# Cross-attention and mixture-of-experts kernel: one-time work of the first batch reordered, shared expert's first products moved among the last batches' second half

## The chip, the cores and the metric

One core of one Trainium2 chip. Time is device microseconds (us) of one launch; less is better. The engines are PE (TensorE, matmuls and transposes), DVE (VectorE), ACT (ScalarE), POOL (GpSimd) and SP (SyncE, which only issues DMAs here). Each has its own instruction stream, written out by hand, and they meet only at semaphores.

## The reference

There are 16 batches of 128 rows of 512 numbers. Each batch passes a cross-attention over 128 context rows (32 heads of 16, rotary positions), and the result is added to the stream. Then a feed-forward layer of one shared expert and 16 routed ones, of which each row takes its two best, is added.

```python
def _swiglu(x, a, b, c):
    return jax.nn.silu(x @ a.T) * (x @ b.T) @ c.T
# attention
q = (x @ Wq).reshape(b, n, N_HEADS, HEAD_DIM)
k, v = jnp.split(ctx @ Wkv, 2, axis=-1)
q = apply_axial_rope(q, pos_map)
k = apply_axial_rope(k, ctx_pos_map)
w = jax.nn.softmax(logits, axis=-1)          # logits = q k^T * scale
attn @ Wout + bout
# feed-forward
shared_output = _swiglu(x, shared_w1, shared_w3, shared_w2)
scores = jax.nn.sigmoid(x @ gate_w.T)
_, topk_idx = jax.lax.top_k(scores + bias, K)
for e in range(E):
    routed_output = routed_output + combine[:, e:e + 1] * _swiglu(x, w1[e], w3[e], w2[e])
# the whole
x = x + attention(layernorm(x), ctx_1024, positions)
x = x + feed_forward(layernorm(x))
```

## The kernel before

Every fp32 product with a weight is made of three fp16 products of a high and a low part. ACT makes the high part of a weight (`weights_high`, `split_shared`: a scaled copy), DVE the low part (`weights_low`, `w13_low`, `w2_low`: the difference). The parts of activations are made in the same way by ACT and by DVE or POOL.

The attention is a software pipeline over batches. `pipeline(step, engine, first, last, ...)` runs `step(b)` for b = 0, 1, 2 and so on, and `on(d, part)` inside it runs that part for batch b + d, if there is such a batch; `ahead` names parts of batch 0 that were issued before the loop. So in step b PE projects k and v of batch b, projects q of batch b - 1 and turns its halves (`stack_transpose`, four groups g; p_st is their one buffer), makes scores, maxima, shifted scores and the weighed values of batch b - 2, the output projection of batch b - 3 (`project_out`), and the transposed second norm and the gate's logits of batch b - 4 (`xn2_transpose`, `gate_logits`). The order of the parts inside a step is fixed for each engine. Batches are counted 0 to 15 here (B = 16), and the last steps, after 15, only drain: PE works to step B + 3 = 19, DVE likewise, ACT and POOL to step 20.

Ahead of the pipeline stands one-time work. SP loads x of batch 0, Wkv, context 0, Wq, context 1, x of batch 1, Wout, x of batches 2 to 15 in one DMA of 3.6 MB (`stream[:, 2:B]`, semaphore `x_late`), the gate's weights and, after two waits, contexts 2 and 3. POOL issues the DMAs of the positions (8 bytes a piece) and of `bout`. DVE normalises batch 0, splits Wkv, splits Wq, clears `negmax`, `hidden` and the value buffer, waits for the positions, makes the angles, waits for ACT's sines and scales the tables; only then does it enter step 0 and 1, in which `k_turn(0)` and `k_sum(0)` rotate the keys. `project_q(0)` on PE waits for `k_turn(0)`, because q and k share the buffer p_qk. Wout is split at the end of step 1, the gate's weights at the end of step 2.

At the seam to the feed-forward part, `split_shared` splits the shared expert's weights in step B + 2 = 18 on ACT and DVE, into `used_twice_too`, which holds keys, queries and values until then. When PE has done step 19 and all logits are kept, it makes the first gate and up products (`gate_up(0, ...)`), and then the slots n = 0 to 15 of the shared expert follow, two to a `pair(j)`: `hidden_transpose(n)`, the gate and up products of n + 1, `down(n)`. PE adds `count()` behind slot 3 (COUNTED) and `place()` behind slot 10 (TABLED); both serve the routing, whose DVE work (`routing_work`) lies beside slots 0 to 11. ACT loads the rows of slot n + 2 with a DMA when the products of slot n + 1 are made (`load_rows`). DVE's first `y_take(0)` waits until SP's first store to `out` has landed, which SP issues when the rows of all batches are stored.

Then 31 tiles at most of two times 128 rows go through the routed experts (slots 16 and on): rows are gathered by POOL, weights loaded by SP, outputs added to `out` by POOL.

## Time and profile before

| | |
|---|---|
| median of 3 runs | 739.29 us (738.96 to 743.66) |
| profiled execution | 740.43 us, of which the span of instructions is 738.7 us |
| mean granted PE clock of the profiled execution | 0.976 of full speed |

The profiled execution's time holds 1.7 us beside its span. The rows from its trace are shown below. Times in them count from the start of the span.

### The profile page before, as it was taken

The numbers are of one execution on the slowest core, as the hardware profiler recorded it, in microseconds if no ns is written. First come the engines' busy times: TensorE is split into PE (matmuls) and PEld (weight loads), VectorE is DVE, ScalarE is ACT, GpSimd is POOL, SyncE is SP. The second block draws the span as 40 slices with busy tenths as digits, with TensorE's granted clock in tenths as the row PEclk, the third lists the DMA queues.
The fourth block names the chain that finished last, engine by engine and source line by source line (L and its number), as shares of the span: only waits on it lengthen the run. The fifth ranks groups of instructions, "written<-read, shape, count | busy, mean of one in ns | idle before, by whom it ended". The sixth has DMA issues, their size and how long they took to land.

```text
span 738.7 us, 20567 instructions
## 1 busy us (share of the span) xinstructions
PE 681.3 (92%) x7616; PEld 436.3 (59%) x7616; DVE 525.3 (71%) x992; ACT 397.6 (54%) x666; POOL 366.1 (50%) x439
## 2 busy tenths in 40 slices
PE   3389999999999999998489998999999999999992
PEld 1156666666666666666245665666666666666661
DVE  5968888888888888876537772467676666767671
ACT  4255666665666666665521111366666656666661
POOL 5455556655556665542100001145776557777662
PEclk9789999999999999999979999999999999999997
DMA  9610111000011110000113256258568875555952
GB/s 300 222 48 9 37 38 39 34 21 35 21 35 35 35 35 28 28 29 31 59 57 100 72 182 225 73 145 250 97 192 239 254 199 94 98 94 78 278 121 31
DMA packets 37601, 73.88 MB, mean 100 GB/s; under 512 B 3920, under 2 KB 8048, under 8 KB 37552
## 3 DMA queue, kind: packets, MB, share of 16 engines
q1 hardware_dynamic: 26736, 48.81, 19.2%
q0 software_dynamic: 8800, 20.73, 14.9%
q10 hardware_dynamic: 2016, 3.67, 1.7%
q8 instruction: 33, 0.54, 0.3%
q14 instruction: 16, 0.13, 0.1%
HBM read 69.85 MB, written 22.81 MB: 125 GB/s over the span
## 4 chain that ended last, share of the span: by engine, by line
PE 83%; DVE 6%; DMA 4%; issue 3%; POOL 2%; ACT 1%; POOLq 0%; SPq 0%; DVEq 0%; ACTq 0%
PE p_sc L712 13%; PE p_qk L692 13%; PE p_sc L692 12%; PE p_v L486 8%; PE p_qk L486 7%; PE p_pv L586 5%; PE p_st L534 4%; PE p_pv L589 4%; PE p_sc L566 3%; PE p_sc L549 3%; PE p_pv L596 2%; PE p_tr L678 2%; PE p_v L699 2%; PE p_sc L569 2%; DMA xeT<-xn2T_dram 2%
## 5 line engine op out<-in xcount | busy, mean ns | idle before, releaser
L809 ACT ACTIVATE prob<-p_sc 128x512 f32<-128x512 f32 x128 | 71.4, 601 | 58.8 <-PE p_sc L569 58.8
L1073 DVE TENSOR_REDUCE negmax<-p_sc 128x4 f16<-128x512 f32 x128 | 82.7, 685 | 8.6 <-PE p_sc L549 8.0
L924 ACT CAST hiddenT<-p_v 128x384 f16<-128x384 f32 x54 | 25.9, 479 | 108.7 <-PE p_v L699 108.7
L712 PE MATMUL p_sc<-used_twice,hiddenT 128*128 128x512 f16 (+1 forms) x342 | 80.1, 379 | 0.0
L1192 DVE TENSOR_TENSOR hidden<-p_sc,act_g 128x352 f32<-128x352 f32 x55 | 28.8, 524 | 68.5 <-PE p_sc L692 47.0
L1467 POOL COPY from_at<-from_rows 128x1 uint32 (+1 forms) x40 | 33.0, 825 | 89.0 <-DVE from_rows L1309 85.8
L692 PE MATMUL p_sc<-used_twice,xeT 128*128 128x352 f16 x468 | 76.2, 313 | 0.0
L692 PE MATMUL p_qk<-used_twice,xeT 128*128 128x352 f16 x468 | 76.2, 312 | 0.0
L1487 POOL DMA_INDIRECT out<-prob,to_at x38 | 67.8, 1786 | 11.0 <-issue 10.1
L1100 DVE SCALAR_TENSOR_TENSOR used_twice<-w,used_twice 128x704 f16<-128x704 f32 x80 | 67.7, 887 | 2.5
L692 PEld LDWEIGHTS p_sc<-used_twice,xeT 128*128 128x128 f16 x468 | 45.8, 98 | 24.0
L486 PE MATMUL p_qk<-used_twice,xnT 128*128 128x512 f16 x192 | 51.7, 396 | 8.5 <-issue 8.5
L912 ACT COPY xeT<-p_tr 128x1024 f16<-128x1024 f16 x40 | 40.5, 1013 | 34.2 <-PE p_tr L678 33.8
L933 ACT ACTIVATE used_twice<-w 128x704 f16<-128x704 f32 x80 | 58.6, 783 | 0.0
L692 PEld LDWEIGHTS p_qk<-used_twice,xeT 128*128 128x128 f16 x468 | 45.7, 98 | 20.5
L1446 POOL TENSOR_TENSOR xn_parts<-xn,xn_parts 128x512 f16<-128x512 f32 x16 | 18.5, 1156 | 70.8 <-ACT xn_parts L836 70.8
L586 PE MATMUL p_pv<-prob,used_twice_too 128*32 128x128 f32 x1024 | 52.6, 277 | 0.5 <-DVE attn L1092 0.5
L1209 DVE TENSOR_SCALAR prob<-p_sc,gate_at 128x512 f32<-128x512 f32 x38 | 28.5, 751 | 33.4 <-PE p_sc L712 30.8
L589 PE MATMUL p_pv<-prob,sum_row 128*32 128x128 f32 x1024 | 51.5, 273 | 0.0
L712 PEld LDWEIGHTS p_sc<-used_twice,hiddenT 128*128 128x128 f16 (+1 forms) x342 | 31.8, 98 | 31.5
L486 PE MATMUL p_v<-used_twice,attnT 128*128 128x512 f16 x192 | 47.6, 380 | 2.0 <-POOL attnT L1442 2.0
L1472 POOL DMA_INDIRECT xe<-xn_dram,from_at x40 | 45.4, 1135 | 8.1 <-issue 3.6
(186 smaller groups left out, 1551.3 us busy)
## 6 DMA issues: line engine op xcount, KB each, us to landing
w<-e SPq DMA_DIRECT2D x20, 1408.0 KB
w<-e SPq DMA_DIRECT2D x20, 512.0 KB
out<-stream SPq DMA_DIRECT2D x17, 256.0 KB, 2.1
xn_dram<-xn_parts SPq DMA_DIRECT2D x16, 256.0 KB, 2.0
xn2T_dram<-xn2T SPq DMA_DIRECT2D x16, 256.0 KB, 2.0
w<-e SPq DMA_DIRECT2D x20, 192.0 KB
stream<-x SPq DMA_DIRECT2D x1, 3584.0 KB, 16.8
xeT<-xn2T_dram ACTq DMA_DIRECT2D x14, 256.0 KB, 2.7
```

The lines of the kernel that those rows point to most:

```text
L486: mm = pe.matmul(to, rows[:, r_part, c, :], w[:, w_part, c, :], start=(c == 0 and r_part + w_part == 0), stop=(c == last and r_part == 1))
L586: pe.matmul(p_pv[2 * HD * n:2 * HD * (n + 1), block], vpad[:, par, head(c, n), :], prob[:, c % RING, n * P:(n + 1) * P], start=(c % 4 == 0 ...
L589: mm = pe.matmul(pv_sum[2 * HD * n:2 * HD * (n + 1), :], sum_row[:, c % 4, :], prob[:, c % RING, n * P:(n + 1) * P], start=False, stop=(c ...
L692: mm = pe.matmul(p_out, xeT[:, u, x_part, c, :], w[:, w_part, c, at:at + INNER], start=(c == 0 and x_part + w_part == 0), stop=(c == KC - ...
L712: mm = pe.matmul(p_y[u][:], hiddenT[0:k, h_part, c, :], w[0:k, w_part, c, :], start=(c == 0 and h_part + w_part == 0), stop=(c == len(ICH) ...
L809: act.activation(prob[:, c % RING, :], p_scored(c)[:], ACT.Exp, scale=SCALE).then_inc(exp_ready, 1)
L912: act.copy(xeT[:, u], p_xT).then_inc(sems.xeT_ready, 1)
L933: act.activation(split[par][0][:, 0, c], w13[:, par, c], ACT.Copy, scale=W_SCALE).then_inc(hi13, 1)
L1073: dve.tensor_reduce(negmax[:, c % 2, at:at + CH], p_scored(c)[:].rearrange("p (h t) -> p h t", t=P), AX_X, ALU.max, negate=True).then_inc( ...
L1100: dve.scalar_tensor_tensor(to[0][:, 1, c], w13[:, par, c], W_SCALE, to[0][:, 0, c], ALU.mult, ALU.subtract).then_inc(lo13, 1)
L1472: pool.indirect_dma_start(out=xe[:, u].rearrange("p a d -> p (a d)"), out_offset=None, in_=xn2_dram, in_offset=bass.IndirectOffsetOnAxis(a ...
L1487: pool.indirect_dma_start(out=out, out_offset=bass.IndirectOffsetOnAxis(ap=to_at[:, par, u:u + 1], axis=0), in_=ye[:, par, u], in_offset=N ...
```

## The change

In the first batch:

- POOL's DMA of the positions goes to ACT's queue, from an array laid out by row, so each of the 128 pieces is one run of 128 bytes.
- DVE clears its buffers first, before x has landed, makes the angles behind the first norm and ahead of the split of Wkv, and splits Wq after the tables; `k_turn(0)` and `k_sum(0)` are issued before step 0. ACT makes the sines ahead of its copies of Wq.
- Wout is split at the end of step 2 in place of step 1. `bias_add` goes one step later, with the wait for `bout` ahead of its first call only.
- SP loads context 2 ahead of the large DMA of x, with two waits before it.

At the seam:

- The shared expert's split weights stand in `used_twice`, where the projections' weights were. Their places with `wo16`, `parts` and the routing tables are exchanged. They are split in three places: gate and up weights on ACT at the end of step 17, on DVE half there and half in step 18, the down weights in step 18.
- PE leaves the pipeline after step 17. It makes the first gate product, spreads the last sums, makes the first up product, and then does `xn2_transpose(14)` and `project_out(15)`. `gate_logits(14)`, `xn2_transpose(15)` and `gate_logits(15)` go into slots 0 and 1, with the work of DVE and ACT that belongs to them.
- `p_u`, `p_hT`, `p_rank`, `p_total` and `p_table` change their PSUM buffers.
- The routing's DVE work begins two slots later, its last piece (`tables`) one slot later; `count()` stands behind slot 5 and `place()` behind slot 11. SP loads the rows of slots 0 and 1 in step 12 in place of step 15.

```diff
-COUNTED, TABLED = 3, 10
+COUNTED, TABLED = 5, 11
-        split = {0: split_in(used_twice[:, 0:each]), 1: split_in(used_twice[:, each:2 * each]),
-                 "shared": split_in(used_twice_too[:, 0:each])}
+        split = {0: split_in(used_twice_too[:, 0:each]), 1: split_in(used_twice[:, each:2 * each]),
+                 "shared": split_in(used_twice[:, 0:each])}
...
             sp.dma_start(wo_in, wo.rearrange("(c p) n -> p c n", p=P)).then_inc(w_o, 16)
+            sp.wait_ge(ctx_lo, 1)
+            sp.wait_ge(ctx_loaded, 2 * 16)
+            sp.dma_start(ctx_sb[:, 0], ctxT[2].rearrange("(c p) t -> p c t", p=P)).then_inc(ctx_loaded, 16)
             sp.dma_start(stream[:, 2:B, :], x_t[:, 2:B, :]).then_inc(x_late, 16)
...
-            load_ctx(2, 0)
...
-            pipeline(step, pe, 0, B + 3, 6, (B - 6) // 2, ahead=[xn_transpose])
+            pipeline(step, pe, 0, B + 1, 6, (B - 6) // 2, ahead=[xn_transpose])
...
+                    following = (n + 1, 1, j, par, kinds[0]) if u == 0 else (n + 1, 0, j + 1, 1 - par, kinds[1])
                     hidden_transpose(n)
-                    if u == 0:
-                        gate_up(n + 1, 1, j, par, kinds[0])
-                    elif kinds[1]:
-                        gate_up(n + 1, 0, j + 1, 1 - par, kinds[1])
+                    if following[-1]:
+                        gate(*following)
+                        if kinds[0] == "shared" and n < 2:
+                            gate_logits(B - 2 + n, n)
+                        up(*following)
                     if kinds[1] == "routed":
                         rows_transpose(n + 2, u, j + 1)
                     down(n, u, j, par, kinds[0])
+                    if kinds[0] == "shared" and n == 0:
+                        xn2_transpose(B - 1, 1)
...
-            pe.wait_ge(logits_kept, B)
             pe.wait_ge(turned_q, B * 3)
+            pe.wait_ge(lo13, KC)
+            gate(0, 0, 0, 0, "shared")
+            spread_recip(B - 1, 1, 1)
+            pe.wait_ge(negT_ready, B)
+            up(0, 0, 0, 0, "shared")
+            xn2_transpose(B - 2, 0)
+            for c in range(KC):
+                project_out(B - 1, 1, c)
...
...
+            act.dma_start(pos_sb[:], pos).then_inc(pos_loaded, 16)
             weights_high(wkv16, wkv_in, KCC, w_kv)
             ctx_high(0, 0)
             xnT_copy(0, 0)
-            weights_high(wq16, wq_in, KC, w_q)
...
+            weights_high(wq16, wq_in, KC, w_q)
...
+                if isinstance(b, int) and b == B + 2:
+                    split_shared2()
                 on(-1, xnT_copy)
                 on(-2, qT_copy, 1)
                 on(-3, summed_v_copy, 1)
                 on(-4, xn2_high)
+                if isinstance(b, int) and b == B + 2:
+                    gate_act(0)
                 on(-1, k_high)
                 on(-2, kT_copy)
                 on(-3, attnT_high)
...
+                if isinstance(b, int) and b == B + 1:
+                    split_shared13()
...
                 gate_act(n + 1)
+                if kinds[0] == "shared" and n == 0:
+                    keep_logits(B - 2, 0)
+                    xn2_high(B - 1, 1)
...
                     load_rows(n + 2, 0)
...
+                if kinds[0] == "shared" and n == 0:
+                    xn2T_copy(B - 1, 1)
                 hT_high(n + 1)
...
                     gate_act(n + 2)
+                if kinds[0] == "shared" and n == 0:
+                    keep_logits(B - 1, 1)
+                    scores_of_experts()
...
+                if isinstance(b, int) and b == B + 2:
+                    split_shared13((2, 3))
                 on(-3, sums_invert, 0)
                 on(-1, k_turn)
                 on(-3, normalise, 0)
                 on(-4, ln2_norm)
+                if isinstance(b, int) and b == B + 2:
+                    split_shared2()
...
+                if isinstance(b, int) and b == B + 1:
+                    split_shared13((0, 1))
...
             hidden_make(0)
+            residual(B - 1, 1)
+            ln2_stats(B - 1, 1)
...
                     hT_low(n)
+                    if kinds[0] == "shared" and n == 0:
+                        ln2_norm(B - 1, 1)
```

## Rows read from the trace of the kernel before

**Rows 1.** The page, part 1: busy time, share of the span, instructions.
```profile
PE 681.3 (92%) x7616; PEld 436.3 (59%) x7616; DVE 525.3 (71%) x992; ACT 397.6 (54%) x666; POOL 366.1 (50%) x439
```

**Rows 2.** Timeline, 0 to 40 us: start, us, engine, line, count, [idle before, releaser].
```profile
11.89 2.59 DVE L1028 SCALAR_TENSOR_TENSOR used_twice<-w,used_twice 128x512 f16<-128x512 f32 x4 [0.96 <-ACT used_twice L848]
15.34 1.76 DVE L1122 MEMSET used_twice_too<- 128x2048 f32 x1 [0.38 <-issue]
23.90 0.75 DVE L1045 TENSOR_TENSOR swp<-p_qk,sin_t 128x256 f32<-128x256 f32 x2
24.75 5.28 PE L486 MATMUL p_qk<-used_twice,xnT 128*128 128x512 f16 x12 [8.53 <-issue]
26.59 4.92 DVE L1028 SCALAR_TENSOR_TENSOR used_twice<-w,used_twice 128x512 f16<-128x512 f32 x4 [0.76 <-ACT used_twice L848]
33.42 0.69 DVE L986 BATCH_NORM_STATS2 stats<-stream 128x6 f32<-128x512 f32 x1
34.43 0.68 DVE L1065 COPY used_twice_too<-p_st 128x1024 f16<-128x1024 f16 x1
37.65 1.03 PE L534 MATMUL p_st<-ident,used_twice 128*128 128x128 f16 x8 [3.27 <-POOL used_twice L1430]
```

**Rows 3.** DMA issues: count, KB each, median us to landing.
```profile
out<-stream SPq DMA_DIRECT2D x17, 256.0 KB, 2.1
stream<-x SPq DMA_DIRECT2D x1, 3584.0 KB, 16.8
```

**Rows 4.** Windows: length, busy of PE, PEld, DVE, ACT, POOL; clock, DMA, GB/s.
```profile
22.00:24.00 2.00, 0.00 (x0) 0.00 (x0) 1.89 (x8) 0.00 (x0) 0.57 (x2) 0.50 1.05 387
```

**Rows 5.** Timeline around 50 us, step 3 begins (DVE, then ACT).
```profile
49.10 0.69 DVE L1040 TENSOR_TENSOR rot<-p_qk,cos_t 128x512 f32<-128x512 f32 x1
...
51.74 1.08 ACT L809 ACTIVATE prob<-p_sc 128x512 f32<-128x512 f32 x2
```

**Rows 6.** Timeline, 346 to 378 us, the last batches (ACT, DVE, POOL, PE).
```profile
346.63 1.09 ACT L809 ACTIVATE prob<-p_sc 128x512 f32<-128x512 f32 x2 [2.95 <-PE p_sc L569]
...
351.70 0.95 DVE L1086 RECIPROCAL recip<-summed_v 128x128 f32<-128x128 f32 x1 [1.84 <-ACT summed_v L815]
...
359.38 1.15 POOL L1442 TENSOR_TENSOR attnT<-attn,attnT 128x512 f16<-128x512 f32 x1 [1.20 <-ACT attnT L821]
...
360.59 2.76 PE L486 MATMUL p_v<-used_twice,attnT 128*128 128x512 f16 x12 [1.73 <-POOL attnT L1442]
...
377.13 1.28 ACT L918 ACT_TABLE_LOAD   x1 [3.39 <-PE p_qk L692]
```

**Rows 7.** The chain that ended last, 355 to 383 us: start, us, what.
```profile
355.67 0.26 PE p_pv L589 x8
...
357.47 0.73 PE p_pv L596 x4
...
360.09 3.56 DVE used_twice_too L1100 x4
...
372.59 0.50 PE p_tr L486 x12
...
373.35 3.70 PE p_qk L692 x12
377.05 2.64 PE p_sc L692 x12
...
380.91 1.79 PE p_qk L692 x12
```

**Rows 8.** Windows at the seam, columns as in rows 4.
```profile
370.00:373.00 3.00, 1.45 (x20) 1.16 (x20) 0.00 (x0) 1.01 (x1) 0.39 (x1) 0.50 0.23 87
```

**Rows 9.** Timeline of PE, 445 to 455 us: slots 10 and 11.
```profile
445.35 1.96 PE L692 MATMUL p_qk<-used_twice_too,xeT 128*128 128x352 f16 x12 [1.43 <-DMA xeT<-xn2T_dram]
...
450.89 0.22 PE L734 MATMUL p_pv<-used_twice,prob 128*128 128x124 f16 x1
...
454.99 1.96 PE L692 MATMUL p_qk<-used_twice_too,xeT 128*128 128x352 f16 x12 [0.94 <-DMA xeT<-xn2T_dram]
```

More of the change, by code:

```diff
@@ L679, in rows_transpose, with rows_by, gate @@
                 mm.then_inc(sems.xeT_done, 1)
-            def gate_up(n, u, j, par, kind):
+            def rows_by(w, p_out, at, u):
+                for c in range(KC):
+                    for x_part, w_part in PARTS:
+                        mm = pe.matmul(p_out, xeT[:, u, x_part, c, :], w[:, w_part, c, at:at + INNER],
+                                       start=(c == 0 and x_part + w_part == 0), stop=(c == KC - 1 and x_part == 1))
+                return mm
+            def gate(n, u, j, par, kind):
                 if kind == "shared":
@@ L687, in gate_up, with up @@
                     pe.wait_ge(lo13, split_no(j) * KC)
-                w = split["shared" if kind == "shared" else par][0]
-                for p_out, at, done in ((p_g, 0, sems.g_done), (p_u, INNER, sems.u_done)):
-                    for c in range(KC):
-                        for x_part, w_part in PARTS:
-                            mm = pe.matmul(p_out, xeT[:, u, x_part, c, :], w[:, w_part, c, at:at + INNER],
-                                           start=(c == 0 and x_part + w_part == 0), stop=(c == KC - 1 and x_part == 1))
-                    mm.then_inc(done, 1)
+                rows_by(split["shared" if kind == "shared" else par][0], p_g, 0, u).then_inc(sems.g_done, 1)
+            def up(n, u, j, par, kind):
+                rows_by(split["shared" if kind == "shared" else par][0], p_u, INNER, u).then_inc(sems.u_done, 1)
             def hidden_transpose(n):
@@ L918, in gate_act @@
                 act.activation(act_g[:], p_g, ACT.Silu, scale=1 / W_SCALE).then_inc(sems.act_ready, 1)
+            pipeline(step, act, 0, B + 2, 6, (B - 6) // 2, ahead=[ctx_high, xnT_copy])
+            xn2T_copy(B - 2, 0)
             def hT_high(n):
@@ L1150, in _ @@
             dve.wait_ge(tables_ready, 2)
+            weights_low(wq16, wq_in, KC, KCC)
+            k_turn(0, 0)
+            k_sum(0, 0)
             def step(b, on):
@@ L1412, in bias_add @@
             def bias_add(b, par):
+                if not later(b, 1):
+                    pool.wait_ge(w_bout, 16)
                 pool.wait_ge(ln1_step, b * 4 + 4)
@@ L1457, in step @@
                 on(-2, q_double)
-                on(-1, bias_add)
+                on(-2, bias_add)
                 on(0, ctx_low)
```

94 lines of the change are left out of this document (45 added, 49 removed).

## The prediction, made before the changed kernel was run

> **What bounds the kernel now.** I read the page first: PE is busy for 681.3 of 738.7 us, so only three kinds of place are worth a change, those where PE isn't busy [rows 1]. The mean hides where they lie, so next came the chain that ended last, cut into the start, the seam between attention and feed-forward, and the routed part, and then the timeline around each gap.
>
> At the start PE sits idle for 8.53 us until its projection of batch 0's queries at 24.75, and again for 3.27 us until the first turned queries at 37.65 [rows 2]. DVE is the engine that it waits for. Between 14.48 (the end of the Wq split, 11.89 + 2.59) and 24.65 (the end of `k_turn(0)`, row at 23.90) DVE does one-time work in a row. The clearing ends at 17.10.
>
> At the seam PE finishes weighing the last values at 355.93 and starts the gate product of slot 1, from which on it runs without a gap, at 380.91: 24.98 us [rows 7]. The chain there is a string of small steps on all engines, with 3.56 us for the low parts of the shared weights in it, and it ends in a first gate product that takes 3.70 us where the next takes 1.79. In between, from about step 3 to step 17, and in the slots, PE is full and a change off PE is worth nothing.
>
> **The start, term by term.** Three pieces leave DVE's string before `k_turn(0)`: the clearing (17.10 less 14.48, 2.6 us) goes to where DVE waits for x, the angles and the wait for the sines go ahead of the Wkv split or beside it, and the statistics of batch 1 (1.0 us of it lies before `k_turn(0)`) go behind. By the trace from 17.10 to 23.90 the second group is worth up to 5 us; against that the angles now stand ahead of the Wkv split and push it back by 0.5 to 1.5 us. `k_turn(0)` should end at 16.6 to 18 in place of 24.65, and `project_q(0)` start 7 to 8 us earlier.
>
> That isn't what decides the gain, because the next thing in DVE's order is late then: `ln1_stats(2)`, which stands ahead of `kT_copy(0)`, waits for the 3.6 MB of x. They were issued at 9.1 and took 16.8 us, so they landed at 25.9 [rows 3]; in the old kernel nobody noticed, as the statistics of batch 2 came at 33.42 [rows 2]. The DMA engines are full in that stretch (busy share 1.05, 387 GB/s [rows 4]), so the DMA of context 2 in front adds its own 128 KB, 0.3 us, and its two waits (to about 11.6) cost nothing as long as Wout's 1 MB still fills the queues. x lands at 26.3. Statistics to `kT_copy(0)`'s end took 33.42 to 35.11, 1.7 us: `kT_copy(0)` ends at 28.1. The other branch, `q_turn(0)` to doubled queries, is ready by my sum at 25.7 to 28.1, by PE's clock in `project_q(0)` (5.28 us at half clock). So the first turned queries start at about 28.15 in place of 37.65: 9.5 us gained. Bounds: 5.5 (x at 30, if the queues run dry before it) to 10.
>
> From this the Wout split is to be taken off. It moves from step 1, where it ended 1.4 us after `project_q(0)`, to the end of step 2, directly ahead of `q_turn(1)` at 49.10 on DVE. Behind that stand q's high part on ACT and the exponential at 51.74, which PE waits for [rows 5]. Nothing covers it: the split costs its four instructions, 2.6 us as at 11.89, or 4.9 us as at 26.59 [rows 2]. I take 2.6, since POOL waits for queries then, as it had little to do at 11.89; ACT's copies (2.2 us) fit into ACT's wait before the first exponential. Start: 9.5 - 2.6 = 6.9 us gained, bounds 1 and 8.
>
> The slow rows have POOL at work beside DVE, as the 4.92 us of the Wout split against 2.59 us of the same shape [rows 2]. The Trainium skill (SBUF — State Buffer, section "SBUF: two separate sides") says why: DVE instructions with two SBUF inputs and POOL's share a port pair by an exclusive lock, and the later one waits for the whole instruction. By that rule the moved split is dear wherever POOL is busy beside it; the sum for the start would be 4.6 us and not 6.9.
>
> Loading positions from ACT's queue, `bias_add` a step later and context 2 earlier have one answer: each takes a wait off POOL or ACT and adds none that anyone stands behind. If the positions landed late all the same, DVE would wait for them before the Wkv split; 2 us are hidden behind the arrival of x.
>
> **The seam, term by term.** ACT makes the high parts of gate and up (four copies, 2.8 us) after step 17's work, in its wait of 2.95 us before the exponential at 346.63 [rows 6]; `xn2T_copy(13)` is squeezed, which costs 0 to 0.3. DVE makes two low parts (1.8 us) before the residual of batch 14 and two before `sums_invert(15, 0)` at 351.70, where it waited 1.84 us for ACT [rows 6]. The down weights fit between 354.3 and 356.4 in the same way. If that cover fails, each 0.1 us of lateness at 351.70 costs 0.1, as that row is on the chain. The 3.56 us on the chain [rows 7] are gone.
>
> PE then goes: gate(0) from 355.93, 1.79 us, to 357.72; `spread_recip(15, 1)`, whose input is there at 357.43, 0.73, to 358.45; up(0) 1.79 and `xn2_transpose(14)` 0.45, to 360.7. Beside them run the normalisation 0.44, ACT's first Silu 0.47 and high part 0.63, POOL's low part 1.15 [rows 6] with 0.1 between, so `project_out(15)` can start at 361.1; with a table load of 1.28 us in front of the Silu [rows 6] and late, at 361.6. I take 361.1. It takes 2.76 [rows 6], the hidden transposes 0.4, and gate(1) starts at 364.2 in place of 380.91: 16.7 us.
>
> Three pieces of PE work that stood ahead of 380.91 now come behind it: `gate_logits` twice at 0.50 [rows 7] and eight transposes, 0.45: 1.4 us back. One wait is new. DVE's `y_take(0)` waits for the first store to `out`; SP issues it behind the rows of batch 15, which are made in slot 0 now. `residual(15)`, statistics, norm, high and low part, transposes and copy put that issue at 371.7, landing 2.1 us later [rows 3]. Behind `y_take(0)` on DVE stand `hT_low(1)` and `hidden_make(2)`, and PE wants the former for `down(1)` at 374.6; it gets it at about 375.4. Cost 0.8 us once, bounds 0 and 3. The extra switch to Exp and back for the gate's scores costs two table loads on ACT (1.28 us each), under gate and up products of 1.79: nothing, at worst 1 us. Seam: 16.7 - 1.4 - 0.8 = 14.5 us, bounds 10.5 and 16.
>
> The first gate product of the feed-forward part ran at half clock: the granted clock is 0.50 from 370 to 373, after five idle microseconds [rows 8], and gate(0) and up(0) took 3.70 + 2.64 us for what takes 2 x 1.79 later [rows 7]. In the new order they follow the weighing, where the clock was full, and I count them at 1.79. The Trainium skill (TensorE: Matmul & The Clock Gate, section "Part 1: The HAM clock gate") has the same: half rate is the state of an idle array, and activity releases it. If the gaps at the seam still let it fall, the sum would be 2.8 us worse.
>
> **The slots.** In slot 10 the gate product of slot 12 waits for its rows until 454.99. Most of that wait is filled by `place()`, which begins at 450.89 and lasts to 453.5, so only 0.94 us is left over [rows 9]. The rows' DMA (issued at 447.36) shares the queues with an expert's weights, which SP issues behind the same slot as before. With `place()` behind slot 11, the wait is 3.6 us bare, and the 2.6 us of `place()` come on top one slot later: a loss of 2.6. Bounds 0 (the rows arrive sooner) and 3.6. `count()` has no such wait beside it; two slots later it costs the same 4.4 us. The gathers start one slot later and still have two slots. The routed part follows PE and shifts as a whole.
>
> **Sum.** 6.9 + 14.5 - 2.6 = 18.8 us. The span becomes 719.9, the profiled execution 721.6 with the 1.7 us around it. That execution stood 1.1 us above the median, so the median to expect is 739.3 - 18.8 = 720.5.
>
> **Rivals.**
> - The start gives little: x of the later batches lands at 30 or the Wout split meets POOL, or both. For it: the queues are full until 25.9, and SP now waits twice before it issues x. Against it: Wout still fills the queues until 15. That takes 5 us off the 6.9: 725.5.
> - The seam has a chain of its own: the store behind `y_take(0)`, rows of slot 2 whose load stands behind batch 15's norm on ACT, or a cold clock. For it: ACT and DVE keep a strict order, and four new pieces stand ahead of what PE needs in slots 0 to 2. Against it: each has slack by my sum. It costs 4, 724.5.
> - `place()` costs nothing, as the rows of slot 12 come sooner in the new order: 718.
> - Slower than before: the clock. PE's stretch after the seam is entered with many short gaps; if the granted clock stayed at its lower level, 1.2 GHz, each slot of 5.9 us would take about 11. From the fourth such slot on the gain of 18.8 us is eaten, and the time is above 740, at 745 for five. Against it: from 380 us on the old kernel is at full clock, after a seam with longer gaps.
> - The change doesn't do what it says: the last steps of the attention are bound elsewhere and the early splits delay them as much as they save later. Then only 6 to 8 us are left: 732.
>
> **How the numbers follow.** Forecast 720.5 with a chance of 0.50, its own range 717 to 724. Start gives little 0.16, seam chain 0.14, `place()` free 0.12, only the small rest 0.05, slower 0.03. The range from 713.5 to 728 leaves out the last two and the ends of two more. Within 1% (7.4 us), about what a measurement of this kernel can tell from no change, or slower lies only in the last two: faster by over 1% 0.93, within 1% 0.04, slower 0.03.
>
> **What would show it.** In the new trace: `project_q(0)` at 17 to 18 and DVE's statistics of batch 2 waiting for the DMA of x until 26.3; four DVE splits of Wout just ahead of `q_turn(1)` and the exponential behind it late by them; gate(0) at once behind the last weighing; gate(1) 6.9 + 16.7 us earlier, at about 357; a wait of DVE before `y_take(0)`; a wait of 3.6 us for rows in slot 10. I am wrong if PE has a new gap of over 2 us in steps 16 to 19, or if the first turned queries come after 31.

## The result, and the profile after

The changed kernel takes 717.75 us, median of five executions (716.59 to 722.21), the kernel before 740.13 (738.96 to 743.66) beside it: ratio 0.969, 95% interval 0.965 to 0.973, so 22.4 us less. The profiled execution is the slowest of the five (722.21 us, span 720.2). First the page, the line that answers to [rows 1]:

```profile
span 720.2 us, 20582 instructions
...
PE 675.9 (94%) x7616; PEld 435.0 (60%) x7616; DVE 522.3 (73%) x992; ACT 399.7 (55%) x668; POOL 365.9 (51%) x438
```

**The start.** The timeline of all engines, answering to [rows 2]:

```profile
1.76 1.76 DVE L1148 MEMSET used_twice_too<- 128x2048 f32 x1 [0.37 <-issue]
...
17.39 0.81 PE L488 MATMUL p_qk<-used_twice,xnT 128*128 128x512 f16 x3 [1.32 <-DVE swp L1077]
...
25.71 2.13 POOL L1475 TENSOR_TENSOR used_twice<-used_twice,ones 128x1024 f16<-128x1024 f16 x1
27.09 0.69 DVE L1018 BATCH_NORM_STATS2 stats<-stream 128x6 f32<-128x512 f32 x1 [3.35 <-DMA stream<-x]
28.11 0.68 DVE L1097 COPY used_twice_too<-p_st 128x1024 f16<-128x1024 f16 x1
28.94 1.01 PE L536 MATMUL p_st<-ident,used_twice 128*128 128x128 f16 x8 [3.77 <-DVE used_twice_too L1097]
...
39.13 2.49 DVE L1060 SCALAR_TENSOR_TENSOR used_twice<-w,used_twice 128x512 f16<-128x512 f32 x4
41.67 0.68 DVE L1072 TENSOR_TENSOR rot<-p_qk,cos_t 128x512 f32<-128x512 f32 x1
44.30 1.08 ACT L824 ACTIVATE prob<-p_sc 128x512 f32<-128x512 f32 x2
44.95 0.23 PE L568 MATMUL p_sc<-used_twice_too 64*128 64x128 f16 x2 [2.15 <-ACT prob L824]
46.92 2.69 PE L488 MATMUL p_qk<-used_twice,ctx 128*128 128x512 f16 x6
```

`project_q(0)` starts at 17.39 in place of 24.75, the statistics of batch 2 now wait for x, and the first turned queries come at 28.94 in place of 37.65: 8.7 us. Wout's split stands in front of `q_turn(1)`, which gains 7.4. PE waits 2.15 us for the exponential behind it and then does the keys' projection in 2.69 us, where the same six products took 1.47 before. The windows (columns as in [rows 4]) show the granted clock, a mean of its two levels of 1.2 and 2.4 GHz, at 0.67 of full speed from 45 us on:

```profile
42.00:45.00 3.00, 0.85 (x21) 0.51 (x12) 2.89 (x9) 1.22 (x3) 0.53 (x1) 1.00 0.68 207
45.00:48.00 3.00, 3.00 (x51) 1.86 (x52) 0.82 (x2) 1.94 (x4) 2.92 (x3) 0.67 1.04 409
```

It is 0.76 in the next three microseconds and 1.00 from 51 us. From the first spread on each step of one kernel lasts as long as the same step of the other, to 0.01 us (20.07 us for two batches in the steady part). So what the start gave can be read off anywhere in the attention: the last values are weighed at 349.95 in place of 355.93, 5.98 us.

**The seam.** The chain that ended last (columns as in [rows 7]):

```profile
349.69 0.26 PE p_pv L591 x8
...
352.28 0.46 ACT act_g L937
352.74 0.62 ACT attnT L836
353.37 0.07 issue
353.43 1.17 POOL attnT L1487
354.60 0.04 issue
354.65 2.76 PE p_v L488 x12
357.41 0.33 PE p_pv L704 x3
357.74 1.79 PE p_qk L686 x12
...
365.47 2.34 DMA out<-stream
...
367.90 0.38 DVE stream L1244
368.28 0.23 issue
368.51 0.56 DVE hiddenT L1236
369.07 0.14 issue
369.20 2.10 PE p_sc L717 x9
```

gate(1) starts 7.8 us after the last weighing where it took 24.98, with the clock at 1.00 throughout; the string of small steps is gone. The first store to `out` is on the chain and leaves the one stall that was foreseen, 0.97 us. The place where both kernels' work is even again is the hidden transpose of slot 2: 371.15 against 392.13, 20.98 us, hence 15.0 for the seam.

**The slots.** The timeline answering to [rows 9]:

```profile
413.03 0.41 SPq L445 DMA_DIRECT2D w<-e  x1
413.12 0.35 ACTq L967 DMA_DIRECT2D xeT<-xn2T_dram  x1
...
417.73 1.97 PE L686 MATMUL p_qk<-used_twice,xeT 128*128 128x352 f16 x12 [0.64 <-DMA xeT<-xn2T_dram]
```

There is no wait of 3.6 us; 0.64 is the whole of it, and it is for the rows of slot 10. The rows of slot 12, for which I had the 3.6 us, are on time. Their issue (`xeT`, from ACT) and that of the second expert's weights (`w<-e`, from SP), before:

```profile
445.47 0.40 SPq L443 DMA_DIRECT2D w<-e  x1
...
447.36 0.33 ACTq L944 DMA_DIRECT2D xeT<-xn2T_dram  x1
```

and after, with the gate product that uses them:

```profile
425.64 0.33 ACTq L967 DMA_DIRECT2D xeT<-xn2T_dram  x1
...
426.22 0.40 SPq L445 DMA_DIRECT2D w<-e  x1
...
429.45 1.95 PE L686 MATMUL p_qk<-used_twice,xeT 128*128 128x352 f16 x12
```

The weights went out 1.9 us ahead of these rows and now go out 0.6 us behind them. Both issues moved, counted from the hidden transpose of slot 10 (443.43 before, 423.26 changed). ACT issues the rows when the gate product of slot 11 is made, and that one had waited 1.43 us itself before [rows 9]: 3.9 us became 2.4. SP issues the weights behind a store that follows `y_take()` on DVE, and a routing step of 2.2 us now stands ahead of it: 2.0 us became 3.0. With the first expert's weights it went the other way. They were 0.9 us behind the rows of slot 10 and are now 0.1 ahead, which is the wait of 0.64.

Before, the slots lost 1.6 and 1.2 us to late rows, beside their 5.85 us and `place()`; now they lose 0.8. From the hidden transpose of slot 2 to that of slot 12 it takes 66.46 us in place of 68.40, so the slots give 1.9 where I had them lose 2.6.

**The routed part.** Of the 22.9 us (5.98 + 15.0 + 1.94) the profiled execution keeps 18.5. The rest goes in one stall; POOL's timeline, then PE's:

```profile
542.40 0.69 POOL L1529 TENSOR_TENSOR carrier_pool<-minus_half 128x1 f32<-128x1 f32 x1 [4.19 <-DMA out<-prob,to_at]
...
551.93 0.90 POOL L1529 TENSOR_TENSOR carrier_pool<-minus_half 128x1 f32<-128x1 f32 x1 [4.11 <-DMA out<-prob,to_at]
...
563.70 0.62 PE L680 MATMUL p_tr<-ident,xe 128*128 128x128 f16 x8 [3.18 <-DMA xe<-xn_dram,from_at]
```

POOL waits for a scatter-add to `out` to land, twice in a row over 4 us, the gather behind it on the same queue is late, and PE runs dry for 3.18 us; with the slower products behind the gap, slots last 5.0 us over the usual 6.30, against 0.75 in the kernel before. The two waits alone don't explain it: the kernel before has two in a row as well (4.27 and 4.01 us), and its PE waits 0.49 us. No run shows that the change causes it either. In the fourteen kernels profiled here the time from the hidden transpose of slot 12 to the end is 277.3 to 278.9 us in eight and 282.6 to 284.0 in six, and both sorts come with old and new orders (the kernel before 278.1, changed 282.6; the late sort in one of four kernels with the old seam and five of ten with the new, too few to tell). The medians stand for the change; a single execution is up to 6 us off.

### The profile page after: what moved, and what is told of

Same layout as the page of the kernel before. It is cut to its first block, busy times and chain, and to the rows that moved or that the text cites. A ratio compares the mean times of both kernels' runs of the same rounds, so it can differ in the third digit from the quotient of the medians.

```text
span 720.2 us, 20582 instructions
## 1 busy us (share of the span) xinstructions
PE 675.9 (94%) x7616; PEld 435.0 (60%) x7616; DVE 522.3 (73%) x992; ACT 399.7 (55%) x668; POOL 365.9 (51%) x438
## 4 chain that ended last, share of the span: by engine, by line
PE 83%; DMA 7%; DVE 3%; issue 3%; POOL 1%; ACT 1%; POOLq 0%; SPq 0%; DVEq 0%
PE p_sc L717 13%; PE p_qk L686 12%; PE p_st L686 11%; PE p_v L488 9%; PE p_qk L488 8%; PE p_pv L588 5%; PE p_st L536 4%; PE p_pv L591 4%; PE p_sc L568 3%; PE p_sc L551 3%; PE p_pv L598 2%; PE p_tr L680 2%; DMA stream<-x 2%; PE p_pv L704 2%; PE p_sc L571 2%
## 5 line engine op out<-in xcount | busy, mean ns | idle before, releaser
L946 ACT CAST hiddenT<-p_pv 128x384 f16<-128x384 f32 x54 | 25.9, 479 | 106.6 <-PE p_pv L704 104.1
L717 PE MATMUL p_sc<-used_twice,hiddenT 128*128 128x512 f16 (+1 forms) x306 | 72.9, 384 | 1.0 <-DVE hiddenT L1236 1.0
L686 PE MATMUL p_qk<-used_twice,xeT 128*128 128x352 f16 x420 | 68.4, 313 | 0.6 <-DMA xeT<-xn2T_dram 0.6
L686 PE MATMUL p_st<-used_twice,xeT 128*128 128x352 f16 x420 | 68.4, 312 | 0.0
L1232 DVE TENSOR_TENSOR hidden<-p_st,act_g 128x352 f32<-128x352 f32 x55 | 28.8, 524 | 52.9 <-PE p_st L686 32.4
L686 PEld LDWEIGHTS p_st<-used_twice,xeT 128*128 128x128 f16 x420 | 40.9, 98 | 21.3
L1491 POOL TENSOR_TENSOR xn_parts<-xn,xn_parts 128x512 f16<-128x512 f32 x16 | 18.5, 1158 | 69.0 <-ACT xn_parts L851 69.0
L686 PEld LDWEIGHTS p_qk<-used_twice,xeT 128*128 128x128 f16 x420 | 40.8, 98 | 19.4 <-DMA xeT<-xn2T_dram 0.9
L488 PE MATMUL p_qk<-used_twice,xnT 128*128 128x512 f16 x192 | 49.1, 380 | 1.3 <-DVE swp L1077 1.3
L536 PE MATMUL p_st<-ident,used_twice 128*128 128x128 f16 x512 | 40.0, 222 | 7.2 <-DVE used_twice_too L1097 3.8
L1463 POOL TENSOR_TENSOR used_twice<-rot,used_twice 128x512 f16<-128x512 f32 x16 | 18.6, 1165 | 53.4 <-ACT used_twice L798 53.4
```

The costliest lines, as they stand in the source:

```text
L488: mm = pe.matmul(to, rows[:, r_part, c, :], w[:, w_part, c, :], start=(c == 0 and r_part + w_part == 0), stop=(c == last and r_part == 1))
L536: mm = pe.transpose(p_st[:, n, :], parts[:, h:h + 2, :].rearrange("p h k -> p (h k)"), ident16[:])
L686: mm = pe.matmul(p_out, xeT[:, u, x_part, c, :], w[:, w_part, c, at:at + INNER], start=(c == 0 and x_part + w_part == 0), stop=(c == KC - ...
L717: mm = pe.matmul(p_y[u][:], hiddenT[0:k, h_part, c, :], w[0:k, w_part, c, :], start=(c == 0 and h_part + w_part == 0), stop=(c == len(ICH) ...
```

## The experiments

Marks used below: `spread` is the first reciprocal spread of the steady steps (56.53 us before, 50.55 changed); "weighing" the end of the last one by the timeline (355.89 before, 349.90 changed; the chain has both 0.05 later); "seam" the time from there to the hidden transpose of slot 2 (36.24 before, 21.25 changed); "slots" from there to slot 12's. Seams repeat to 0.03 us in all kernels with the new order and the store in its place.

One execution of each kernel is profiled, and the start isn't the same in each of them. So the experiments on the start are read against all kernels with the same start, not against one. Five have the new start unchanged (the first five rows):

| | first turned queries | negated maxima copied | granted clock, 30 to 36 us | keys' projection | weighing | weighing less turned queries |
|---|---|---|---|---|---|---|
| changed | 28.94 | 38.99 | 0.80 | 2.69 | 349.90 | 320.96 |
| e7 | 28.59 | 38.50 | 0.82 | 2.74 | 349.40 | 320.81 |
| e1 | 28.61 | 39.78 | 0.57 | 1.47 | 349.15 | 320.54 |
| e5 | 28.37 | 39.54 | 0.60 | 1.47 | 348.91 | 320.54 |
| e9 | 28.59 | 39.62 | 0.63 | 1.47 | 348.98 | 320.39 |
| e6 | 27.92 | 38.98 | 0.66 | 1.47 | 348.34 | 320.42 |
| e11 | 28.99 | 40.28 | 0.60 | 1.47 | 347.32 | 318.33 |
| e4 | 30.79 | 41.76 | 0.50 | 1.47 | 348.81 | 318.02 |
| e10 | 31.05 | 42.55 | 0.65 | 2.06 | 353.39 | 322.34 |

The five fall into two sorts. In the changed kernel and e7 the clock is higher ahead of the maxima, which come 1.0 us sooner after the turned queries or more, and lower at the keys' projection behind them. In e1, e5 and e9 it is the other way round. The two nearly cancel: from the turned queries to the weighing the five differ by 0.6 us.

**e1_start: only the new start.** The kernel before, with the new order of the one-time work on DVE, ACT and SP (clearing first, angles ahead of the Wkv split, `k_turn(0)` ahead of step 0, context 2 early, `bias_add` a step later, Wout's split in step 2, positions on ACT's queue); seam and routing old.

> The old kernel with the changes of the first batch alone (positions from ACT's queue, clearing and angles first, Wout split at the end of step 2, context 2 ahead of x, bias a step later). Theory: the start is worth 6.0 us, as the last weighing of the changed kernel stands 5.98 us earlier than before, and nothing later gives it back: 734.1 us against 740.1. Rival (the start's gain is hidden by a later wait for transfers): within 2 us of the old kernel. Rival (the two halves need each other): over 8 us.

Measured 733.25 us (732.41 to 736.88), ratio 0.990 (0.986 to 0.995). `spread` 49.80, weighing 349.15: 6.7 us earlier than before, where the theory had 6.0. The seam takes 35.41.

**e2_seam: all but the new start.**

> The changed kernel with the old order of the first batch. Theory: seam and slots are worth 15.0 + 1.9 us by the changed kernel's trace, so 723 us against 740.1, and gate of slot 1 stands 17.2 us earlier than in the old kernel. By my sum on record it is 14.5 - 2.6 = 11.9 us: 728. Rival (the halves need each other): the sum of this and of the start alone misses 22.4 us by over 4.

Measured 723.34 us (721.40 to 729.49), ratio 0.977 (0.972 to 0.983). `spread` 55.03, though its start is that of the kernel before, 1.5 us earlier than there: from 36 to 45 us the granted clock is 0.72 and then 1.00 here, and 0.61 and then 0.65 there. The seam takes 21.23 us, the slots 66.58. The seam with the routing is the greater part of the gain, and doesn't depend on the start: 7.3 us (e1) and 17.2 make 24.5, against 22.4 for both, within the 4 us set for the rival.

**e3_routing_late: the routing's steps two slots later, nothing else.**

```
-COUNTED, TABLED = 3, 10
+COUNTED, TABLED = 5, 11
-                (0, 0): [(routing_scores,)], (0, 1): [(two_best, range(0, 4))],
+                (2, 0): [(routing_scores,)], (2, 1): [(two_best, range(0, 4))],
```

> The old kernel with only the routing's DVE work two slots later (its last piece one), count() behind slot 5 and place() behind slot 11. My prediction: the wait for the rows of slot 12 stays as it was and is now bare, 3.6 us in slot 10, so hidden_transpose(12) comes 2.6 us later than the old kernel's 460.53. Theory from the changed trace: with y_take(7) no longer late behind routing work, SP issues the first expert weights 1 us earlier beside the rows of slot 10, which costs 0.6 us there, and the rows of slot 12 are then ahead of the second weights and on time; hidden_transpose(12) comes 1.9 us earlier. Rival (the slots' gain came from the seam): no shift, within 0.3 us.

Measured 737.71 us (735.93 to 738.56), ratio 0.995 (0.991 to 0.999). Slots 66.54 in place of 68.40 with the old seam, so it is the shift alone that gains there. The theory came true in its steps: weights 0.03 us ahead of the rows of slot 10 and a wait of 0.72, then 0.6 behind the rows of slot 12 and none. Slots with the old routing took 68.40 and 67.48 (e1), so it is worth 0.9 to 1.9 us. `spread` 54.91: the third kernel with the old start, and 1.6 us before the first.

**e4_wout_in_wait: Wout's split in DVE's wait for x, ACT's copies behind `v_copy(0)`.**

```
+                if isinstance(b, int) and b == 2:
+                    weights_low(wo16, wo_in, KC, KCC + KC)
                 on(0, ln1_stats)
...
                 if isinstance(b, int) and b == 2:
-                    weights_low(wo16, wo_in, KC, KCC + KC)
```

> The changed kernel with the Wout split moved into step 2 between q_sum(0) and the statistics of batch 2, where DVE waits 3.35 us for x, and ACT's copies behind v_copy(0). Theory: the split's 2.5 us and the half-clock k projection behind the gap on PE (2.62 in place of 1.40 us) both go: the last weighing comes 3.0 to 3.9 us earlier than in the changed kernel (349.95), 714 us against 717.8. Rival (another wait takes the split's place, ACT's copies being late or POOL's queries): under 1 us. Rival (the split meets POOL's q_low and q_double in that place and takes 4.9 us): 1.5 to 2.5 us.

Measured 721.92 us (716.05 to 722.82), ratio 0.972; weighing 348.81: 1.1 us earlier than the changed kernel's, but within 0.4 of e1, e5 and e9, so no gain is shown. The timeline of DVE and POOL:

```profile
23.66 5.37 DVE L1061 SCALAR_TENSOR_TENSOR used_twice<-w,used_twice 128x512 f16<-128x512 f32 x4
24.46 1.49 POOL L1465 TENSOR_TENSOR used_twice<-rot,used_twice 128x512 f16<-128x512 f32 x1 [1.28 <-ACT used_twice L798]
26.03 2.45 POOL L1477 TENSOR_TENSOR used_twice<-used_twice,ones 128x1024 f16<-128x1024 f16 x1
```

The same four instructions take 5.37 us in place of 2.49, and POOL's two take 1.49 and 2.45 in place of 1.15 and 2.13. So the split outlasts the wait that was to hide it: the statistics of batch 2 come at 28.95 and the turned queries 1.9 us later than in the changed kernel, and nearly all that the split no longer costs behind them is spent there. The second rival had the mechanism. This is the contention of DVE and POOL that [rows 2] showed (4.92 us).

The Trainium skill (SBUF — State Buffer, section "SBUF: two separate sides") states that a DVE instruction with two SBUF inputs and a GpSimd instruction that reads SBUF take turns at one port pair, each for its whole length. The trace agrees: of the four pieces, 0.68 us long alone, the two begun while POOL was at work took 1.64 and 2.61.

**e11_wout_beside_scores: the same split between the first scores.** Three of its four pieces behind `k_sum(1)`, one behind `row_max(3)`, ACT's copies behind `v_copy(0)`.

```
                 on(-1, k_sum)
+                if isinstance(b, int) and b == 2:
+                    weights_low(wo16, wo_in, KC - 1, KCC + KC)
                 on(-2, row_max, 0)
...
                 on(-2, row_max, 3)
+                if isinstance(b, int) and b == 2:
+                    weights_low(wo16, wo_in, KC, KCC + KC, KC - 1)
```

> The changed kernel with the split of Wout moved out of its place behind negmaxT(0) (2.49 us at 39.13 us, ahead of q_turn(1)) to the gaps of DVE between the first row sums and maxima, where POOL is idle (30.2 to 34.8 us) and DVE waits for scores. My theory: DVE's 2.49 us there are on the start's chain; q_turn(1) moves forward by 2.5 us, the last weighing ends at about 347.4 in place of 349.9, time about 2.5 us under the changed kernel (some 715). Unlike the same split beside POOL's q_low and q_double (5.37 us), it should keep 2.5 us in all. Rival: the pieces delay the row maxima of batch 0 by their own length, so that nothing is gained: last weighing 349.5 to 350, same time.

Measured 715.23 us (713.26 to 715.76), ratio 0.963 (0.957 to 0.968); weighing 347.32, 2.6 us earlier. The timeline:

```profile
30.75 1.89 DVE L1061 SCALAR_TENSOR_TENSOR used_twice<-w,used_twice 128x512 f16<-128x512 f32 x3
...
36.57 0.94 DVE L1061 SCALAR_TENSOR_TENSOR used_twice<-w,used_twice 128x512 f16<-128x512 f32 x1
...
45.57 1.47 PE L488 MATMUL p_qk<-used_twice,ctx 128*128 128x512 f16 x6
```

The size came out, in part by luck. Against the changed kernel the exponential behind `q_turn(1)` starts 1.1 us earlier (43.17, 44.30), and the rest is the keys' projection (1.47, 2.69). But e1, e5 and e9 have that short projection with the old place of the split, and PE's wait of 2.15 us too. Against those three, which share e11's clock, the way from the turned queries to the weighing is 2.1 to 2.2 us shorter: that is what moving 2.5 us of split gives. The fourth piece met POOL and took 0.94 us in place of 0.68.

**e10_clear_late: the clearing back behind the Wq split.**

```
-            dve.memset(negmax[:], 0.0)
-            dve.memset(hidden[:], 0.0)
-            dve.memset(used_twice_too[:, 0:4 * DIM], 0.0).then_inc(zeroed, 1)
...
             weights_low(wq16, wq_in, KC, KCC)
+            dve.memset(negmax[:], 0.0)
...
             k_turn(0, 0)
```

> The changed kernel with the clearing (three fills on DVE, some 2.6 us) back behind the Wq split, ahead of k_turn(0). My theory: the batch-2 statistics wait 3.35 us for x at 27.09, so of 2.6 us only what exceeds the slack of the other branch counts: k_turn(0) ends 2.6 us later, q_double (ready at 27.84 us) at 30.4, the first turned queries at about 30.5 in place of 28.94, the last weighing about 1.5 us later (351.4). Rival: the clearing is hidden whole behind the DMA of x, no change; second rival: the longer idle time drops the clock and project_q(0) takes 5.28 in place of 2.75 us, then the turned queries come 4 us later.

Measured 721.46 us (718.09 to 722.46), ratio 0.973; weighing 353.39, 3.5 us later than in the changed kernel, 4.1 later than the mean of the five. The second rival won: the clock fell. But the turned queries come 2.1 us later, not 4; the rest is lost behind them, at a clock of 0.65 from 30 to 36 us and 0.64 from 48 to 51. PE's row and the window of it:

```profile
19.50 5.28 PE L488 MATMUL p_qk<-used_twice,xnT 128*128 128x512 f16 x12 [3.70 <-DVE swp L1077]
```

```profile
21.00:24.00 3.00, 3.00 (x8) 1.06 (x7) 1.44 (x2) 0.58 (x2) 2.70 (x3) 0.50 1.05 390
```

With 3.70 us of idle time ahead of it the projection runs at the lower level (granted 0.50, 1.2 GHz) and takes 5.28 us; in the changed kernel 1.32 us of idle time precede it, the clock is 1.00, and it takes 2.75. Moving 2.6 us of fills was thus worth 3.5 to 4.5 us, by which of the five it is read against, over half of the start's gain.

**e6_x2_own: batch 2's rows of x in a DMA of their own.**

```
+            sp.wait_ge(x_early, 2 * 16)
+            sp.dma_start(stream[:, 2:3, :], x_t[:, 2:3, :]).then_inc(x_early, 16)
-            sp.dma_start(stream[:, 2:B, :], x_t[:, 2:B, :]).then_inc(x_late, 16)
+            sp.dma_start(stream[:, 3:B, :], x_t[:, 3:B, :]).then_inc(x_late, 16)
```

> The changed kernel with the rows of x of batch 2 in a DMA of their own, directly behind batch 2's context, instead of at the head of the long one of 15.69 us. My theory: stats(2) at 27.09 us waits 3.35 us for that DMA; with its own one it starts without a wait, and the first turned queries then follow POOL's q_double (end 27.84 us) at about 28.0 in place of 28.94: the end of the last score weighing (349.9) moves by 0.5 to 1 us. Rival: the turned queries of the first three batches are not what sets the pace (the scores wait for PE's own queue of projections), and nothing moves by over 0.3 us; or the transfers share the same engines so that the rows land no earlier.

Measured 715.38 us (714.21 to 721.42), ratio 0.965; weighing 348.34. The timeline of DVE and PE:

```profile
23.70 0.68 DVE L1020 BATCH_NORM_STATS2 stats<-stream 128x6 f32<-128x512 f32 x1
...
27.92 1.03 PE L538 MATMUL p_st<-ident,used_twice 128*128 128x128 f16 x8 [1.51 <-POOL used_twice L1477]
```

The wait is gone and the turned queries come 1.0 us earlier than in the changed kernel, 0.45 to 0.7 earlier than in e1, e5 and e9. Read against the changed kernel alone, nothing seems left of it at the negated maxima (38.98, 38.99), as the rival has it. That is the clock: the changed kernel is of the other sort. Against the three of e6's sort the maxima come 0.6 to 0.8 us earlier and the weighing 0.6 to 0.8, so all of it arrives, and the theory holds. Of the 1.56 us to the changed kernel's weighing 1.0 is the earlier turned queries, the rest the clock. So x's arrival does bind the start, as predicted.

**e7_seam_old_order: splits in their new places, products of slot 0 back behind the attention.** The expectation speaks of the routing at its old place; the edit leaves it at its new one, and the slots take 66.63 us.

```
-            pipeline(step, pe, 0, B + 1, 6, (B - 6) // 2, ahead=[xn_transpose])
+            pipeline(step, pe, 0, B + 3, 6, (B - 6) // 2, ahead=[xn_transpose])
...
+            pe.wait_ge(logits_kept, B)
             gate(0, 0, 0, 0, "shared")
-            spread_recip(B - 1, 1, 1)
             pe.wait_ge(negT_ready, B)
             up(0, 0, 0, 0, "shared")
-            xn2_transpose(B - 2, 0)
-            for c in range(KC):
-                project_out(B - 1, 1, c)
```

> The changed kernel, new start, new places of the weight splits, but with the first shared products put back behind the last batch's projection, and the routing at its old place. My theory: the seam's gain of 15.0 us is made of two: the splits' place (they no longer stand between project_out(15) and gate(0)) about 2 us, the interleaving about 13 us. From the last weighing to gate(1): 24.86 us before, 7.7 us changed, here about 22.9. Time about 731 us. Rival: the splits were what the first gate waited for, so that moving them alone gives most of it: from the last weighing to gate(1) about 12 us, time about 720.

Measured 734.19 us (729.79 to 738.62), ratio 0.987 (0.980 to 0.995). From the weighing to gate(1) 24.29 us by the timeline (24.86 before), not 22.9; the seam is 35.66, no shorter than the three with the splits on the chain (36.24, 35.41 in e1, 35.65 in e3). PE's projection of the last batch in e7, its first gate product there, and the projection in e1:

```profile
354.10 5.30 PE L488 MATMUL p_v<-used_twice,attnT 128*128 128x512 f16 x12 [1.73 <-POOL attnT L1468]
...
367.59 3.18 PE L686 MATMUL p_qk<-used_twice,xeT 128*128 128x352 f16 x12 [0.48 <-ACT logits L874]
```

```profile
353.86 5.30 PE L488 MATMUL p_v<-used_twice,attnT 128*128 128x512 f16 x12 [1.73 <-POOL attnT L1446]
```

`project_out(15)` takes 5.30 us at half clock here and in e1, 4.31 in e3, and 2.76 before [rows 6]. At half clock it covers the splits: from its start to the next transposes e1, with the splits, and e7, without, both take 10.39 us. Where the projection was shorter, 2.76 us before and 4.31 in e3, the same stretch took 9.86 in both, so there the splits set it. At full clock e7's stretch would last 7.9 us, an estimate from 10.39 less 5.30 plus 2.76, and the splits' new places would give 2.0; no run shows that. As it ran, they give nothing that can be seen in this order. They give room for the interleaving, and that is worth 14.4 (35.66 less 21.25), of which about 2.5 are the full clock in `project_out(15)`.

**e5_out_early: the first store one step earlier.**

```
                 if isinstance(b, int) and b == B - 4:
+                    sp.dma_start(out[T:T + P], stream[:, 0, :]).then_inc(out_stored, 16)
                     sp.wait_ge(xn2T_stored, 2 * 16)
...
-            sp.dma_start(out[T:T + P], stream[:, 0, :]).then_inc(out_stored, 16)
```

> The changed kernel with one edit: the first store of the output rows of the last batches (the one that y_take(0) waits 5.67 us for, and through it down(1) 0.97 us) is issued one step earlier. My theory: the seam's only stall is that wait. hT_copy(2) minus hT_copy(0) goes from 13.90 to about 12.9 us, the wait of 0.97 us ahead of down(1) is gone, time about 1 us under the changed kernel's 717.75 (ratio to before near 0.967). Rival: down(1) waits for hiddenT as well, so the difference stays at 13.9 and the time is the same within 0.3 us.

Measured 717.01 us (714.93 to 721.32), ratio 0.965; seam 20.10 in place of 21.25, and PE's row for down(1) has no wait:

```profile
367.07 2.11 PE L717 MATMUL p_sc<-used_twice,hiddenT 128*128 128x512 f16 x9
```

The wait was for the store alone. Its 1.1 us are clear on the trace and too little to be seen in the medians.

**e9_rows_first: expert weights behind the rows.**

```
+                    sp.wait_ge(sems.xT_loaded[0], (j + 2) * 16)
```

> The changed kernel with SP issuing the expert weights of each of the first two weight loads only once the rows of the next slot pair have landed. My theory of the slots: what gate(n) waited for before was the transfer of its rows sharing the DMA engines with weights issued ahead of them; in the changed kernel one such pair is left (0.64 us). With the rows first that stall is gone: hT_copy(12) minus hT_copy(2) goes from 66.46 to 65.8 us. Rival: the rows are late because of their own issue, then 66.4 stays; and if the weights land late instead, their split or the first routed slots stall and more than 66.46 is shown.

Measured 723.00 us (719.09 to 724.14), ratio 0.975 (0.971 to 0.979), slots 67.87: worse. The stall of slot 10 is gone and slot 11 has a longer one. The timeline of the queues and PE:

```profile
415.76 0.41 SPq L445 DMA_DIRECT2D w<-e  x1
...
418.05 0.33 ACTq L968 DMA_DIRECT2D xeT<-xn2T_dram  x1
...
424.06 1.96 PE L687 MATMUL p_qk<-used_twice,xeT 128*128 128x352 f16 x12 [2.04 <-DMA xeT<-xn2T_dram]
```

The wait put the weights 3.6 us behind the rows of slot 10 in place of 0.1 ahead, and so 2.3 ahead of the rows of slot 11. In these traces rows issued 0.6 us before an expert's weights are on time, rows issued 0.1 behind the first of its three transfers make PE wait 0.64, and rows issued about 2 behind, with all three out, 2.0 here; before the change such rows came 3.6 us late, most of it under `place()`. My theory was right on the cause and wrong on the cure.

**e8_all and e12_three: the edits together.** e8_all has the edits of e11, e6, e5 and e9; e12_three leaves e9's wait out.

> The changed kernel with four edits together: Wout's split beside the first scores (worth 2.6 us at the last score weighing by its own run), batch 2's rows of x in their own DMA (by its own run up to 0.7 us net of the scatter between runs), the first store one step earlier (1.1 us less from hT_copy(0) to hT_copy(2)), and the weights of the first two experts behind the rows of slots 4 and 6 on SP. My theory: they lie on different stretches and add up: 2.6 + 0.5 + 1.1 + 0.6 = 4.8 us, time about 713. Rival: the gathers of the routed part, whose stalls vary from run to run, hide it: time within 1 us of 715 like the single edits, with hT_copy(12) 4 to 5 us earlier all the same.

Measured 718.46 us (713.77 to 722.38), ratio 0.968 (0.964 to 0.972). Weighing 346.57, seam 20.11, but slots 69.79: the wait of e9 again, with 2.29 us idle in slot 11 and the gate product behind it at 3.09 us in place of 1.96. The expected 713 was missed, and the rival isn't borne out either: slot 12's transpose is only 1.1 us earlier.

> The changed kernel with three edits together (Wout's split beside the first scores, batch 2's rows of x in their own DMA, the first store one step earlier), without the wait ahead of the expert weights. My theory: the four-part version lost to this wait: its own run and the four-part run show slot 11 waiting 2.04 and 2.29 us for rows, 1.4 and 3.3 us lost from hT_copy(2) to hT_copy(12). Without it that distance is 66.5 us again, hT_copy(12) comes at about 433.2 us, 4.4 us before the changed kernel, and the time is 713.5 us (ratio to before near 0.963). Rival: the earlier store or the transfers' new times bring the slots' stall about, not the wait: then 68 us or more stay, and the time is 715 to 718.

Measured 717.39 us (712.98 to 718.65), ratio 0.965 (0.960 to 0.970). Slots 66.94 and slot 12's transpose at 432.74, 4.9 us before the changed kernel, its span of 711.6 the shortest of all profiled ones; both as expected. The median isn't: two of six executions lie at 713.0 and 713.5, four at 717.2 to 718.7, which looks like the two sorts of the routed part, though only one of the six was profiled. Whether the edits make its late sort more frequent can't be told from six. By the intervals neither this kernel nor e11_wout_beside_scores is shown to beat the changed one; both beat the kernel before.

## Why the prediction was right

It said 720.5 us (713.5 to 728); 717.75 was measured, a gain of 22.4 where I had 18.8. By its steps:

- *The start, 9.5 less 2.6.* The order of events is that of the prediction: `project_q(0)` at 17.39 (17 to 18), the statistics waiting for x to 27.09 (26.3), the turned queries at 28.94 (28.15), four splits ahead of `q_turn(1)` at 2.49 us (2.6). 5.98 us came at the weighing of the profiled pair, 5.6 as the mean of five kernels with the new start (49.55 to 50.55) against three with the old (54.91 to 56.53), where I had 6.9. By these means the turned queries gained 8.8, not 9.5, and behind them 3.2 were lost where I had 2.6. Wout's split took 2.49 of the 3.2. For the other 0.7 nothing but the clock is seen to differ, and my sum has no term for it. The clock also worked the other way, unseen: I gave the clearing 2.6 and it was worth 3.5 to 4.5 (e10), because `project_q(0)` came to 2.75 us from 5.28. That x set the pace was right, up to the weighing (e6).
- *Contention with POOL as a price of Wout's split* didn't come about at the place chosen, where POOL had nothing to do; it did at the place that looked free (5.37 us in e4).
- *The seam, 14.5.* 15.0 for the profiled pair, 14.2 to 15.0 against the three kernels with an old seam. The terms: 16.7 was 17.2, since `project_out(15)` started 4.7 us after the weighing and not 5.2; 1.4 back was 1.0 (first to third hidden transpose, 12.76 us in e5, 11.76 before); the stall put at 0.8 was 0.97, cost 1.1 and vanished with the store (e5). gate(0) and up(0) ran at 1.8 us each. The working holds for one reason less than I gave: the 3.56 us of splits were on the chain before [rows 7], but taking them off alone gave nothing (e7), since `project_out(15)` then ran at half clock.
- *The slots, -2.6.* This is the step that failed: "With `place()` behind slot 11, the wait is 3.6 us bare". `place()` cost its 2.6 (a slot of 8.49 us in place of 5.85), but the rows of slot 12 made nobody wait; what was left was 0.64 us for those of slot 10, worth 0.8. I took the order of two queues' transfers as fixed ("behind the same slot as before"). It wasn't: the weights went out 1.9 us ahead of slot 12's rows before and 0.6 behind them after, and with the routing's steps moved and nothing else the same order and the same gain appear (e3). The rival "`place()` costs nothing" had 0.12 and named this; at 718 it is also nearest to the time. That the total came within 3 us is partly luck: the errors of the slots and of the start have opposite signs.
- *Slower, and only the small rest:* no trace of either. After 361 us the granted clock is 1.00 in every stretch of 6 us but the two behind the gather's stall (0.99 and 0.73), until PE is done.

The missing 3.6 us are thus +4.5 (slots), +0.5 (seam), -0.9 (start), and -0.5 in the scatter between executions.

## What to carry to other kernels

A piece of work is worth its own length plus what the idle time that it causes does to TensorE's clock: 2.6 us of fills cost 3.5 to 4.5, and 3.56 us off a chain gave nothing. One profiled execution isn't a baseline for effects of a microsecond: against one kernel x's own DMA seemed to give nothing at the scores, against three with the same clock all of it arrived. When work is moved on one engine, list the DMA issues of all queues behind it in the new order of time; what counts is which of two transfers is issued first, and rows issued 1.9 us behind the weights came 3.6 us late, rows issued 0.6 ahead of them were on time. Put a split beside an engine's wait only after reading what POOL does in that same wait: beside it the split took 5.37 us in place of 2.49.

## What the runs showed of the hardware

- PE's six products took 1.47 or 2.69 us at the same place in kernels with the same start (47.30 in e1, 46.92 in the changed one), each time after the same wait of 2.15 us. The clock after a gap isn't the same from execution to execution. In the two with 2.7 us it had been higher 12 us earlier, so of the scatter of 1.0 us at the steady steps it leaves 0.6, and the rest is when the turned queries came (28.37 to 28.94).
- The twelve products of `project_out(15)` took 2.76, 4.31 and 5.30 us in three kernels (before, e3, e1) with one and the same order of instructions there.
- POOL waits over 4 us for a scatter-add to land in some slots. The late gather behind such waits cost up to 6.7 us of PE's time (e9, 3.73 of it idle) and nothing in e3, e6 and e11, and this is the difference of 5 us between the two sorts of profiled executions. Two waits in a row over 4 us are in e3 too, so they alone don't decide it; what does stays open.
